# Quantising the FFN tiles two at a time, and the sum over tokens once per sequence

## What is computed

```python
x = x + 0.5 * ffn(layernorm(x))      # FFN 1
x = x + attention(layernorm(x))
x = x + 0.5 * ffn(layernorm(x))      # FFN 2, the same weights

def ffn(x):                          # fp4_linear quantises both operands in blocks of 16
    return fp4_linear(silu(fp4_linear(x, w_gate)) * fp4_linear(x, w_up), w_down)

def attention(x):
    attn = softmax((x Wq' + bq)(x Wk' + bk)' / 16)
    attn = eye + attn
    attn = attn - mean(attn, axis=-1)    # the mean of a row is 2 / 512
    return attn @ x
```

## Time and profile before

| | |
|---|---|
| median of three executions | 2394.25 us (2389.05 to 2400.36) |
| the profiled execution: its time | 2397.43 us |
| its span, first to last instruction | 2395.6 us |
| TensorE (PE) matmul busy | 2099.0 us, 88% |
| VectorE (DVE) busy | 2069.8 us, 86% |
| ScalarE (ACT) busy | 1674.6 us, 70% |
| GpSimd (POOL) busy | 750.7 us, 31% |
| mean granted TensorE clock | 0.969 of full speed |

### The profile page before, as it was taken

How to read it: one execution, slowest core, us unless ns; L and a number is a source line. 1 busy time by engine, 2 the same in 40 slices (tenths; PEclk the granted TensorE clock), 3 DMA queues, 4 the chain that set the end, 5 groups by cost and what they waited for, 6 DMA issues and landing times. The chain is left out here.

```text
span 2395.6 us, 46422 instructions
## 1 busy us (share of the span) xinstructions
PE 2099.0 (88%) x13514; PEld 1249.1 (52%) x13514; DVE 2069.8 (86%) x3961; ACT 1674.6 (70%) x4315; POOL 750.7 (31%) x664
## 2 busy tenths in 40 slices
PE   2678999999999998999989999898999999899875
PEld 1344555555555555555555555555555555555442
DVE  6567998999989898998999899898989989899764
ACT  3357777777777777777777777786777778777641
POOL 3122333332333333233333332333333233333211
PEclk9879999999999999999999999999999999999887
DMA  1233554554445445444544544445454444544432
GB/s 55 42 69 72 93 104 82 101 100 94 95 87 104 94 97 96 95 96 81 109 93 91 96 101 99 91 91 104 91 95 101 95 89 88 103 95 87 90 57 57
DMA packets 741596, 214.25 MB, mean 89 GB/s; under 512 B 706464, under 2 KB 741152, under 8 KB 741408
## 3 DMA queue, kind: packets, MB, share of 16 engines
q1 hardware_dynamic: 741408, 212.54, 45.1%
HBM read 19.53 MB, written 16.78 MB: 15 GB/s over the span
## 5 line engine op out<-in xcount | busy, mean ns | idle before, releaser
L1163 PE MATMUL gu_ps<-wgu_hi,xT 128*128 128x512 f16 (+1 forms) x3072 | 956.9, 366 | 64.5 <-DMA xT<-f_dq 55.0
L586 POOL TENSOR_TENSOR tile_area<-tile_area,h_rs 128x704 f32<-128x704 f32 x256 | 390.3, 1525 | 1291.1 <-DVE h_rs L1076 1291.1
L1163 PE MATMUL gu_ps<-wgu_lo,xT 128*128 128x512 f16 (+1 forms) x1536 | 562.5, 366 | 0.0
L1163 PEld LDWEIGHTS gu_ps<-wgu_hi,xT 128*128 128x128 f16 x3072 | 303.6, 99 | 377.0 <-issue 63.2
L1264 PE MATMUL out_ps<-wd_hi,hT 128*128 128x256 f16 x1536 | 364.0, 280 | 134.8 <-DMA hT<-h_dq 134.8
L1264 PE MATMUL out_ps<-wd_lo,hT 128*128 128x256 f16 (+1 forms) x1536 | 378.4, 281 | 0.0
L959 DVE SCALAR_TENSOR_TENSOR tile_area<-gu_ps,gu_unit,tile_area 128x704 f32<-128x704 f32 x256 | 241.5, 944 | 130.1 <-PE gu_ps L1163 63.7
L851 ACT ACTIVATE tile_area<-gu_ps,gu_unit 128x704 f32<-128x704 f32 x256 | 215.5, 842 | 188.8 <-PE gu_ps L1163 188.4
L706 ACT ACTIVATE h_y<-tile_area 128x704 bf16<-128x704 f32 x256 | 200.3, 782 | 92.2 <-POOL tile_area L586 92.2
L1264 PEld LDWEIGHTS out_ps<-wd_hi,hT 128*128 128x128 f16 x1536 | 153.4, 100 | 203.0 <-issue 120.3
L971 DVE TENSOR_REDUCE h_am<-tile_area 128x44 f32<-128x704 f32 x256 | 227.1, 887 | 6.7
(11 more groups left out here) (169 smaller groups left out, 4090.7 us busy)
## 6 DMA issues: line engine op xcount, KB each, us to landing
x<-in_L_attn_x SPq DMA_DIRECT2D x32, 512.0 KB, 3.9
out<-x_later SPq DMA_DIRECT2D x32, 512.0 KB, 3.6
hT<-h_dq SPq DMA_TRANSPOSE x256, 3.6
pT<-p SPq DMA_TRANSPOSE x128, 3.2
xT<-f_dq SPq DMA_TRANSPOSE x64, 4.3
w_raw<-in_L_ffn_w_down SPq DMA_DIRECT2D x1, 704.0 KB, 7.5
w_raw<-in_L_ffn_w_gate SPq DMA_DIRECT2D x1, 640.0 KB, 4.6
w_raw<-in_L_ffn_w_up SPq DMA_DIRECT2D x1, 640.0 KB, 5.7
```

The costliest lines, as they stand in the source:

```text
L586: g.tensor_tensor(blocks(h_xq[:, n % 2, :], FB), blocks(hid[:, n % 2, :], FB), per_block(h_rs[:, n % 2, 0:FB], FB), ALU.mult).then_inc(xq_ ...
L1163: ins = t_.matmul(dst, x, y, start=(i == 0), stop=(i == len(todo) - 1))
```

## The change

Three things change.

- Two tiles that follow each other are a "duo" (started at odd j). From the block maxima to the dequantised halves VectorE, GpSimd and ScalarE work on both in one instruction, of 1408 columns where there were 704. The silu, `hid`, `h_sh`, `h_sl`, the transposes, the down projection and the residual stay one per tile. GpSimd multiplies in place, on `hid`, which has four buffers. `h_t` and `h_q` have one buffer for a duo, `hT` has four.
- The eight matmuls with constants go from each `attend`. Once per sequence `add_tokens` makes the sum over all tokens (8 matmuls), ScalarE copies it to `token_sum`, GpSimd adds it to the four tiles of `x1`, and the identity's part comes from ScalarE, which replaces `x1` by `x1 * (1 + rstd/SX) + shift/SX` (four instructions of 128x256, with `a_own` made by two small GpSimd instructions).
- The order of every queue and the ages of nearly every step are new. On TensorE the three cuts of `gate_up` are together at the end of a slot; the down projections of a duo are in one slot, five slots after the duo's start, where a tile's was three after its own.

```diff
-A_TURNS = (("q0", "afront", 3), ("q1", "afront", 3))
-OUT_TURNS = (("att0", "query", 5), ("att1", "query", 5), ("down", "tile", 3))
+A_TURNS = (("q0", "afront", 5), ("q1", "afront", 5), ("sum", "afront", 7))
+OUT_TURNS = (("att1", "query", 7), ("down0", "duo", 5), ("down1", "duo", 5), ("att0", "query", 7))
...
+            if "tile" in s.started and j % 2 == 1:
+                start(s, "duo")
...
+        def duo_pairs(ap):
+            return ap.rearrange("p i (b k e) -> p i b k e", k=FP4_BLOCK // 2, e=2)
+
+        def duo_q(ap):
+            return ap.rearrange("p (i b k e) -> p i b k e", i=2, k=FP4_BLOCK // 2, e=2)
+
+        def duo_scale(ap):
+            return ap.rearrange("p (i b) e -> p i b e", i=2).unsqueeze(3).broadcast_to([P, 2, FB, FP4_BLOCK // 2, 2])
...
+                if s.duo[4] is not None:
+                    m = s.duo[4]
+                    pool.wait_ge(rs_done.sem, rs_done.at(m + 1, pair))
+                    g.tensor_tensor(blocks(hid2[:, m % 2, :], 2 * FB), blocks(hid2[:, m % 2, :], 2 * FB),
+                                    per_block(h_rs[:, m % 2, 0:2 * FB], 2 * FB), ALU.mult).then_inc(xq_done.sem, 1)
...
+                if s.afront[7] is not None:
+                    b = s.afront[7]
+                    pool.wait_ge(a_free.sem, a_free.at(turn_sum[b] + 1, pair))
+                    pool.wait_ge(x1_own_done.sem, x1_own_done.at(TILES * (b + 1), pair))
+                    g.tensor_tensor(x1[:, b % 2, :, :], x1[:, b % 2, :, :],
+                                    token_sum[:, :].unsqueeze(1).broadcast_to([P, TILES, D]), ALU.add).then_inc(x1_ready.sem, 1)
...
+                    a_.activation(token_sum[:, :], tr_a[:, 0:D], ACT.Copy, scale=1.0 / (SP * SX)).then_inc(a_free.sem, 1)
...
+                if s.duo[3] is not None:
+                    m = s.duo[3]
+                    act.wait_ge(xq_done.sem, xq_done.at(m + 1, pair))
+                    if pair is not None or m >= 2:
+                        act.wait_ge(q_done.sem, q_done.at(m - 1, pair))
+                    a_.activation(h_y[:, m % 2, :], hid2[:, m % 2, :], ACT.Abs, scale=LIFT).then_inc(lifted.sem, 1)
...
+                    for t in (0, 1):
+                        a_.activation(x1[:, b % 2, t, :], x1[:, b % 2, t, :], ACT.Identity, scale=a_own[:, t:t + 1],
+                                      bias=a_own[:, TILES + t:TILES + t + 1]).then_inc(x1_own_done.sem, 1)
...
+                if s.duo[4] is not None:
+                    m = s.duo[4]
+                    dve.wait_ge(t_done.sem, t_done.at(m + 1, pair))
+                    v.scalar_tensor_tensor(out=h_q[:, :], in0=h_y[:, m % 2, :], scalar=ROUND_MIN,
+                                           in1=h_t[:, :], op0=ALU.max, op1=ALU.subtract).then_inc(q_done.sem, 1)
...
+                    v.tensor_tensor(duo_pairs(h_dq[:, m % 2, :, 0:FF]), duo_q(h_q[:, :]),
+                                    duo_scale(h_sh[:, m % 2, :, :]), ALU.mult).then_inc(dh_done.sem, 1)
...
+                    v.tensor_tensor(duo_pairs(h_dq[:, m % 2, :, FF:2 * FF]), duo_q(h_q[:, :]),
+                                    duo_scale(h_sl[:, m % 2, :, :]), ALU.mult).then_inc(dl_done.sem, 1)
...
             def attend(a, i, turn):
 
-                t = 2 * (a % QPS) + i
                 return products(out_bank(turn), [(pT[:, i, 0, k, :], pT[:, i, 1, k, :], xs_hi[:, k, :], xs_lo[:, k, :])
-                                                 for k in range(TILES)],
-                                [((own_sp if k == t else other_sp)[:, :], xs[:, k, :])
-                                 for k in range(TILES) for xs in (xs_hi, xs_lo)])
+                                                 for k in range(TILES)])
+
+            def add_tokens():
+
+                return products(tr_a[:, 0:D], [], [(other_sp[:, :], xs[:, k, :]) for k in range(TILES) for xs in (xs_hi, xs_lo)])
...
+                if s.duo[5] is not None:
+                    m = s.duo[5]
+                    pe.wait_ge(hT_in[2 * (m % 2)].sem, hT_in[2 * (m % 2)].at(16 * (m // 2 + 1), pair))
+                    if pair is not None or turn_down[2 * m] >= 2:
+                        pe.wait_ge(out_added.sem, out_added.at(turn_down[2 * m] - 1, pair))
+                    down(2 * m).then_inc(out_full.sem, 1)
```

More of the change, by code:

```diff
@@ L88, in schedule @@
     slots = []
-    count = dict(tile=0, query=0, front=0, afront=0)
+    count = dict(tile=0, duo=0, query=0, front=0, afront=0)
     info = {"tile": [], "front": []}
@@ L126, in schedule @@
         for s in slots:
-            items = dict(tile=s.tile, query=s.query, front=s.front, afront=s.afront)
+            items = dict(tile=s.tile, duo=s.duo, query=s.query, front=s.front, afront=s.afront)
             for name, what, age in order:
@@ L234, in macaron_kernel @@
         xT = sb("xT", [P, 2, 2, TILES, DC, P], F16)
[L238 to L252, removed]
+        NG = 12
+        WCOLS = NG * D + DC * FWRAP
+        area = sb("tile_area", [P, WCOLS])
+        h_t = area[:, 0:2 * FF]
+        sg = area[:, 2 * FF:4 * FF].rearrange("p (i f) -> p i f", f=FF)
+        w_t = area[:, 0:WCOLS]
+        hid = sb("hid", [P, 4, FF])
+        hid2 = hid[:, :, :].rearrange("p (i e) f -> p i (e f)", e=2)
+        h_y = sb("h_y", [P, 2, 2 * FF], BF16)
+        h_q = sb("h_q", [P, 2 * FF], F16)
+        h_am = sb("h_am", [P, 2, 2 * FB + 2])
+        h_s = sb("h_s", [P, 2, 2 * FB + 2])
+        h_rs = sb("h_rs", [P, 2, 2 * FB + 2])
+        h_unit = sb("h_unit", [P, 2, 2])
+        h_sigma = sb("h_sigma", [P, 4, 2])
+        h_sh = sb("h_sh", [P, 2, 2 * FB, 2], BF16)
+        h_sl = sb("h_sl", [P, 2, 2 * FB, 2], F16)
+        h_dq = sb("h_dq", [P, 2, 2, 2 * FF], F16)
+        hT = sb("hT", [P, 4, HC, P], F16)
         a_sum = sb("a_sum", [P, TILES])
@@ new lines, in emit @@
+                if s.duo[3] is not None:
+                    m = s.duo[3]
+                    if pair is not None or m >= 4:
+                        act.wait_ge(out_added.sem, out_added.at(max(turn_down[2 * m - 8], turn_down[2 * m - 7]) + 1, pair))
+                    a_.activation(h_sigma[:, m % 4, :], h_s[:, m % 2, 2 * FB:2 * FB + 2], ACT.Copy,
+                                  scale=down_unit[:, :]).then_inc(sigma_done.sem, 1)
+                    act.wait_ge(unit_done.sem, unit_done.at(m + 1, pair))
+                    a_.activation(h_sh[:, m % 2, 0:FB, :], twice(h_s[:, m % 2, 0:FB], FB), ACT.Copy,
+                                  scale=h_unit[:, m % 2, 0:1]).then_inc(sh_done.sem, 1)
@@ L940, in emit @@
+                if s.query[4] is not None:
+                    a = s.query[4]
                     dve.wait_ge(score_full.sem, score_full.at(2 * a + 2, pair))
@@ L1001, in emit @@
[L1001 to L1005 removed]
+                if s.duo[2] is not None:
+                    m = s.duo[2]
+                    dve.wait_ge(am_done.sem, am_done.at(m + 1, pair))
+                    v.tensor_reduce(h_am[:, m % 2, 2 * FB:2 * FB + 2], h_am[:, m % 2, 0:2 * FB].rearrange("p (e b) -> p e b", e=2),
+                                    AX.X, ALU.max).then_inc(hm_done.sem, 1)
@@ L1006, in emit @@
+                if s.front[4] is not None:
+                    f = s.front[4]
                     dve.wait_ge(f_q_done.sem, f_q_done.at(f + 1, pair))
@@ L1086, in _ @@
+                if s.duo[3] is not None:
+                    m = s.duo[3]
+                    dve.wait_ge(lifted.sem, lifted.at(m + 1, pair))
+                    v.scalar_tensor_tensor(out=h_t[:, :], in0=h_y[:, m % 2, :], scalar=ROUND_MIN,
+                                           in1=hid2[:, m % 2, :], op0=ALU.max, op1=ALU.add).then_inc(t_done.sem, 1)
             for u, (at, n) in enumerate(UNITS):
```

898 lines of the change are left out of this document (458 added, 440 removed).

## The result

The changed kernel takes 2505.31 us (2503.06 to 2507.54, median of four runs) against 2395.14 beside it, a ratio of 1.046 (1.044 to 1.048). It is slower, by 110 us, where 2335 us was forecast and 2420 was the upper end.

A forecast was written before the change was run, and what follows sets the result against it. VectorE and TensorE, both at 92%, were taken to bind together: period 69.25 - 2.4 (work) + 0.3 (idle) = 67.15 us, times 32 is 2148.8, plus 179.6 and 8; 2335 us on the median, range 2262 to 2420.

The forecast's parts named there:

- rival D: VectorE's doubled `h_dq` loses the fast rate: 5.6 us more a sequence, period 72.75, time 2514 us; chance 0.06.
- the value taken: GpSimd's product for a duo, at 1.27 ns a column: 2.42 us.
- the estimate of 3.05 us: GpSimd's product for a duo at twice a tile's: the wait grows by 0.6 us, the sum by 20 us.
- where the new order waits: New waits in slots 2, 3 and 6, together 4.0 us, plus 2.0 slack: idle time 5.7 to 6.0, +0.3.
- 1.9 us for `h_y` in slot 2: VectorE waits 1.9 us at `h_t`: 4.0 us chain through GpSimd and ScalarE, 2.1 us of other work.
- 1.5 for `f_xn` in slot 3: VectorE waits 1.5 us at `f_am`, 0.55 before, since GpSimd's queue has `xs_lo` and the front behind the duo's product.
- 0.6 for the scores in slot 6: Scores need the previous query's low halves: TensorE held for about 0.8 us, of which 0.6 comes through.
- 2.0 left over: Slack kept of the present 5.7 us idle time a sequence, as the `hT` and `aT` waits shrink.
- Fill and drain: Time of the span outside the 32 periods: 179.6 us, and 8 more as `down` comes about one slot later.
- A: The forecast itself: both engines' work falls, new waits replace old; 2335 us, between 2290 and 2375; chance 0.44.
- Rival C: Duo's chain through GpSimd and ScalarE adds to old waits, slots 2 and 3; 2434 us; chance 0.31 with milder forms.
- The bound falls about evenly: Work falls on VectorE by 2.4 us and TensorE by 2.6 us a sequence; -2.4 taken for the period.

The follow-up runs named there:

- 1: Changed kernel with GpSimd's addition to `x1` moved in its queue from slot 5 to behind `f_shift` of a later slot; 2440.6 us, ratio 1.018.
- 2: Changed kernel with the addition to `x1` left in place but over one column of each tile, not 256; 2436.0 us, ratio 1.017.
- 5: Timed addition: changed kernel, the addition to `x1` still in slot 5 but starting after VectorE's second `h_dq` has ended; 2435.4 us, ratio 1.017.
- 8: On top of 6, VectorE makes the low parts of `p` of a sequence's first query ahead of `h_am` in slot 5; 2386.3 us, ratio 0.995.
- 4: Kernel before without its 32 matmuls with constants a sequence (identity and mean left out); 2335.8 us, ratio 0.975.
- 3: Changed kernel's duos and new order, but the identity by 32 matmuls again, no addition, no scaling of `x1`; 2438.9 us, ratio 1.018.
- 12: As 11, with GpSimd's addition cut in four, a tile each behind its products, the first also behind `s_mneg`; 2354.2 us, ratio 0.983.
- 11: Kernel before with only the sum once a sequence, `x1` scaled by ScalarE, GpSimd's whole addition behind its product in slot 2; 2413.6 us, ratio 1.011.
- 6: On top of 5, ScalarE's second pair of squares for the attention moved from slot 1 to slot 0; 2423.8 us, ratio 1.013.
- 9: On top of 8, ScalarE takes silu ahead of `xs_hi` and `h_sh` ahead of the squares; 2395.9 us, ratio 0.999.
- 10: On top of 9, ScalarE takes `h_y` ahead of the second pair of squares; 2574.7 us, ratio 1.074.

## Why the prediction was wrong

**The work was nearly right.** The steps are as forecast: `h_dq` 0.81 us to the next start (0.79 forecast; rival D is out), `h_am` 1.53, `h_t` 1.65 up to the dependent `h_q`. VectorE without the collision does 61.1 us a sequence (61.1 forecast), TensorE 61.7 in the kernel with the timed addition (about 61). The savings are smaller than forecast, 2.1 us for 2.4 on VectorE, whose start was 63.2 over ten whole sequences and not 63.6, and 2.0 for 2.6 on TensorE, where each matmul left out took 0.08 us off the busy time and not its step of 0.11. `hT` fell to 0.9 us in 1200. GpSimd's product takes 2.59 us, 0.17 over the value taken and well inside its bounds; the estimate of 3.05 us by the Trainium skill's page "GPSIMD Engine Reference" is 0.46 over it.

**The first failed step: "where the new order waits" priced the waits for semaphores alone.** The addition to `x1` was counted as 2 us on an engine with room, and an overlap with VectorE's work that costs nothing was taken for granted. It costs 65 to 70 us of the 110 (experiments 1, 2, 5). The trace of before had the signs. The earlier trace rows show `f_shift`, four elements, at 0.36 us, where it takes 0.20 undisturbed, and the tile view of `h_dq` there (shortest, median, longest ns) has a longest of 0.93 us for a median of 0.52:

```profile
L980 DVE TENSOR_TENSOR h_dq<-h_q,h_sl x138: 510/516/930, 603.8 to 1792.0; 128x704 f16<-128x704 f16 x138
```

Nine of these 138 take 0.88 us or more, one in every second sequence, each begun while GpSimd's `xs_lo` ran. This one started at 1020.00, and the `xs_lo` in the earlier trace rows runs from 1018.36 to 1020.49:

```profile
1020.00 0.88 DVE L980 TENSOR_TENSOR h_dq<-h_q,h_sl 128x704 f16<-128x704 f16 x1
```

**The second: the new waits were put too low, at the wrong instructions.** Forecast were 1.9 us for `h_y` in slot 2, 1.5 for `f_xn` in slot 3, 0.6 for the scores in slot 6, and 2.0 left over: 6.0. Measured, in a sequence: slot 2 3.9 (of it 0.6 for `h_y`), slot 3 0.55, slot 6 3.0, the back edge 1.3, which was there before, the rest 0.95: 9.7. In slot 2 the chain was looked at from `h_rs` through the product; ScalarE's queue of the attention's scaling, sums and squares stands ahead of silu and `h_sh` there, and holds `hid` and `h_sl` first. The forecast also took the 35.4 us of the earlier trace rows for silu as they stood; two thirds of them were the back edge. In slot 6 the scores wait for the low parts of `p`, which stand behind a duo's `h_am`, `h_s` and `h_rs` in VectorE's queue; 8 took out 1.3 us of these 3.0 and the period fell by 1.26.

**The sum.** Period: 67.15 + 2.16 (stretched `h_dq`) + 3.7 (idle) = 73.0. Fill and drain were 23 us less than forecast, which hides a little of it. Two prices of rivals were added up wrongly and decide nothing: D's eight `h_dq` are 8 x 0.77 = 6.2 us by its own steps, not 5.6, and A's upper bound comes to 2380 us, not 2375.

**Rival C has the number of what is left, but not its places.** Without the collision the duos' order takes 2435 us at a period of 70.5, where C said 2434 at 70.25: VectorE is idle for 9.4 us (70.5 - 61.1), 3.4 more than before, as C had it. But C put the waits at `h_t` in slot 2 and `f_am` in slot 3, behind the chain from `h_rs` through GpSimd's product. There VectorE waits for 0.6 and 0.55 us, where it waited for 0.2 and 0.6 before. The new idle time is at silu and `h_sh` in slot 2 and in slot 6. That the total agrees to 1 us is luck in good part. "The bound falls about evenly" failed too: TensorE's relief, worth 1.4 us a sequence in the old order (4), shows no gain in the new (3 against 5).

**The two parts of the change apart.** On the kernel before, the sum once a sequence brings -1.7% if GpSimd's addition is placed well (12), +1.1% if not (11). The duos with their order cost +1.8% (3). Together, without the collision, +1.7% (5); the gain of the one is lost in the other. In the best order found for both together it is -0.5% (8). Not shown: how much of the duos' loss is their double latency and how much only the new order of the queues, as no kernel here has one without the other. Experiment 8 shows that at least 1.3 us of a period was order. Why the squares in slot 0 (6) moved silu by 0.3 us and not by 1.7 is argued from GpSimd's rows and not tried by itself.

## What to carry to other kernels

Work moved to an engine "with room" must be checked against its neighbour's instructions of that moment, instruction by instruction: where a VectorE instruction had both inputs in SBUF, it and GpSimd's ran one at a time here, and the loss was what was left of the one that came first (0.88 us became 3.04, and 0.22 became 2.31, beside an addition of 2.36). Cut the long one in pieces (11 against 12), or tie it by a semaphore to a stretch in which the neighbour reads PSUM or reduces (5). And a wait taken out of an order in which such pairs are only kept apart by that wait can cost more than it brings (9, 10): look at durations against their minimum, not at waits alone. When a wait's named releaser ended long before the wait did, as silu at the back edge, something else ended it.

## What was not expected of the hardware

- An instruction on 128x2 elements took 2.06 and 2.31 us instead of 0.22 beside GpSimd's addition of 2.36 us; GpSimd's `f_rstd` on 128x4 took 2.39 instead of 1.0 beside `h_t` and `h_q`. The profile counts all of it as busy time.
- GpSimd's product took 1526 ns for 704 columns before and 2589 for 1408, in place, after: 1.51 ns a column. The line through 704 and the 1024 columns of `f_xq` gave 1.27. Why `f_xq` lies below the line through the two products isn't shown.
- The back edge of the loop costs VectorE 2.6 to 2.7 us in every second sequence, in the kernel before as in the changed one, and once 4.3 with the old identity (3).
- Behind 12 of 16 waits of TensorE of 2.86 us its granted clock was 0.50.
